# The second attention's projections as four products of 64 rows and 64 columns in two banks, with queries and keys sent apart

## The reference, cut to what matters

```python
def _L1_attn_ref(x, Wqkv, bqkv, Wr, br):        # x: [16, 512, 256], H = 16 heads of HE = 16
    xh = x.reshape(b, c, h, he).transpose(0, 2, 1, 3)
    qkv = jnp.einsum('bhce,ef->bhcf', xh, Wqkv) + bqkv      # Wqkv: [16, 48], the same for every head
    q, k, v = jnp.split(qkv, 3, axis=-1)
    att = jnp.einsum('bhqe,bhke->bhqk', q, k) / jnp.sqrt(jnp.float32(he))
    mask = jnp.tril(jnp.ones((c, c)), k=-1)
    att = jax.nn.softmax(att * mask, axis=-1)               # masked scores are 0, not left out
    out = jnp.einsum('bhqk,bhke->bhqe', att, v)
    return out.transpose(0, 2, 1, 3).reshape(b, c, d) @ Wr + br
```

## Time and profile before

| what | value |
|---|---|
| median of 3 runs | 2801.84 us (2799.59 to 2802.47) |
| profiled execution | 2797.78 us |
| its span | 2796.0 us |
| TensorE busy | 2615.3 us (94%) |
| VectorE, ScalarE, GpSimd busy | 2280.6, 2078.2, 1811.9 us |

### The profile page before, as it was taken

One profiled execution on the slowest core, in us unless ns is written; L12 is line 12 of the kernel. 1 busy time (PEld: TensorE's weight loads), 2 busy tenths in 40 slices (PEclk: granted clock), 3 DMA queues, 4 the chain that ended last, 5 costly groups with the idle time before them and its releaser, 6 DMA issues. The chain is left out here.

```text
span 2796.0 us, 75274 instructions
## 1 busy us (share of the span) xinstructions
PE 2615.3 (94%) x27044; PEld 1818.8 (65%) x27044; DVE 2280.6 (82%) x6931; ACT 2078.2 (74%) x3782; POOL 1811.9 (65%) x3152
## 2 busy tenths in 40 slices
PE   5999999999999999997889789999999999699999
PEld 3677777777777777775333257777777777466766
DVE  5999999999999999986655468888888888488998
ACT  4998899999998999895333257667677776478886
POOL 3767666777667766774421157677777767588885
PEclk8999999999999999999899889999999999899999
DMA  4334433444334433441000166655556664000001
GB/s 116 68 62 77 79 61 62 74 80 79 61 64 80 73 61 62 72 72 47 10 0 1 32 106 105 105 96 104 97 101 97 104 99 71 1 16 24 24 24 39
DMA packets 110387, 182.21 MB, mean 65 GB/s; under 512 B 27008, under 2 KB 96384, under 8 KB 97920
## 3 DMA queue, kind: packets, MB, share of 16 engines
q1 hardware_dynamic: 106560, 176.61, 34.7%
q10 hardware_dynamic: 3456, 0.79, 0.2%
HBM read 116.25 MB, written 60.29 MB: 63 GB/s over the span
## 5 line engine op out<-in xcount | busy, mean ns | idle before, releaser
L808 POOL TENSOR_TENSOR ratio_scores<-ratio_scores,ratio_max_cols 128x512 f32<-128x512 f32 (+3 forms) x1024 | 726.1, 726 | 319.3 <-DVE ratio_max_cols L718 316.9
L1328 DVE CUSTOM_DVE_ANT_0 zeroed_unused<-bank,zeroed_drop 128x512 bf16<-128x512 f32 (+3 forms) x1024 | 440.0, 484 | 121.1 <-PE bank L198 120.9
L198 PE MATMUL bank<-ratio_k_stack,ratio_q_stack 102*128 102x512 bf16 (+7 forms) x2048 | 506.3, 303 | 33.4 <-DVE ratio_max_cols L718 17.5
L718 DVE CUSTOM_DVE_ANT_0 ratio_scores<-bank,ratio_scores 128x512 f32<-128x512 f32 (+3 forms) x1024 | 472.4, 489 | 22.2
L1216 ACT ACTIVATE zeroed_prob<-bank 128x512 f32<-128x512 f32 x640 | 370.1, 593 | 161.2 <-PE bank L1103 160.3
L580 ACT ACTIVATE ratio_prob<-bank 128x512 f32<-128x512 f32 x640 | 378.4, 592 | 105.5 <-PE bank L494 102.7
L708 DVE TENSOR_TENSOR ratio_scores<-bank,ratio_inverse 128x512 f32<-128x512 f32 x640 | 435.9, 681 | 16.8 <-PE bank L198 9.6
L491 PE MATMUL bank<-const_f_sb,ratio_scores 128*128 128x128 f32 x2560 | 409.9, 274 | 0.9 <-ACT ratio_prob L580 0.9
L569 ACT ACTIVATE ratio_inverse<-bank 128x512 f32<-128x512 f32 x640 | 381.1, 596 | 12.7 <-PE bank L201 12.6
L573 ACT ACTIVATE ratio_inverse<-ratio_inverse 128x1024 f32<-128x1024 f32 x320 | 338.6, 1058 | 10.1
L1446 POOL TENSOR_SCALAR_AFFINE_SELECT zeroed_prob<-zeroed_prob 128x256 f32<-128x256 f32 (+1 forms) x640 | 227.7, 361 | 178.0 <-ACT zeroed_prob L1216 172.2
(11 more groups left out here) (178 smaller groups left out, 5412.6 us busy)
## 6 DMA issues: line engine op xcount, KB each, us to landing
ratio_q_stack<-ratio_parts_q SPq DMA_DIRECT2D x186, 128.0 KB
ratio_k_stack<-ratio_parts_k SPq DMA_DIRECT2D x186, 128.0 KB
zeroed_q_stack<-zeroed_parts_q SPq DMA_DIRECT2D x186, 128.0 KB, 4.7
zeroed_k_stack<-zeroed_parts_k SPq DMA_DIRECT2D x186, 128.0 KB, 7.7
ratio_parts_q<-ratio_parts SPq DMA_DIRECT2D x96, 128.0 KB
ratio_parts_k<-ratio_parts SPq DMA_DIRECT2D x96, 128.0 KB
zeroed_parts_q<-zeroed_parts SPq DMA_DIRECT2D x96, 128.0 KB
zeroed_parts_k<-zeroed_parts SPq DMA_DIRECT2D x96, 128.0 KB
```

The lines of the kernel that those rows point to most:

```text
L198: i = e.matmul(bank[:, off:off + w], qs[0:rows, s, hh, ib * P:(ib + 1) * P], ks[0:rows, s, hh, 0:w], start=(k == 0), stop=mask is None, sk ...
L718: i = e.tensor_tensor_reduce(seg, dot_banks[n % 2][:, at], seg, 1.0, 0.0, ALU.mult, ALU.max, mx[:, pair % M_BUFS, c:c + 1])
L808: i = e.tensor_tensor(seg, seg, mx[:, pair % M_BUFS, c:c + 1].to_broadcast([P, w]), ALU.subtract)
L1328: i = e.tensor_tensor_reduce(unused[:, n % 2, at], bank[:, at], drop[:, L - (ib + 1) * P:L], 1.0, 0.0, ALU.add, ALU.max, mx[:, pair % FOLD ...
```

## The change

- `project` issues four products of 64 rows and 64 columns: the weight's two diagonal blocks (heads 0 to 3, heads 4 to 7) times the two halves of the tokens. Heads 0 to 3 go to `prep_bank`, heads 4 to 7 to `o_bank`, the bank of the attend step; the first 256 tokens to partitions 0 to 63, the others to partitions 64 to 127. `values` issues eight products with 64 rows, a 128-column stationary operand and 64 moving columns, into the same two banks.
- Readers of these results read two banks, in two instructions each: ScalarE's and VectorE's `split`, VectorE's `values`.
- The products wait until the groups begun before them have been copied out of `o_bank`, and the attend step waits until projections issued before it have been read.
- The parts lie differently in their tile (tokens over partitions, heads over columns), so `send_parts` issues six DMAs of 64 partitions for a side, in runs of 512 bytes.
- SyncE gathers the queries before it sends the keys: send queries, gather queries, send keys, gather keys.
- New slots: queries of the half after the next at 13, keys of the next half at 3 (before: 11 and 15 for the half after the next), values at 5 (3), turns at 8 and 11 (6 and 9), suffix sums at 17 (19), tails at 9 (7). For half 1: queries at slot 1 and keys at 3 (before 1 and 5). ScalarE and VectorE do their steps of the split ahead of the rest of their preparation; the steps still follow one slot apart.

```diff
-Z_ROOT_AT, Z_XN_AT, Z_TURN_AT, Z_VALUES_AT, Z_SUFFIX_AT = 0, (3, 6), (6, 9), 3, 19
-Z_SPLIT_AT, Z_REST_AT, Z_MID_AT, Z_LO_AT = (11, 15), (12, 16), (13, 17), (14, 18)
+Z_ROOT_AT, Z_XN_AT, Z_TURN_AT, Z_VALUES_AT, Z_SUFFIX_AT, Z_SPLIT_AT = 0, (5, 8), (8, 11), 5, 17, (13, 3)
+Z_REST_LAG, Z_MID_LAG, Z_LO_LAG = 1, 2, 3
+QUARTER = HALF // 2
-Z_SECOND_AT, Z_SECOND_REST_AT, Z_SECOND_MID_AT, Z_SECOND_LO_AT = (1, 5), (2, 6), (3, 7), (4, 8)
-Z_TAILS_AT = 7
+Z_SECOND_AT = 1
+Z_TAILS_AT = 9
...
+def split_at(n, halves):
+
+    half, at = divmod(n, HALF_UNITS)
+    if n == Z_SECOND_AT:
+        return 1, 0
+    if at == Z_SPLIT_AT[0] and half + 2 < halves:
+        return half + 2, 0
+    if at == Z_SPLIT_AT[1] and half + 1 < halves:
+        return half + 1, 1
+    return None, None
...
+    two_banks = lambda n: max(prep[use] for slot, use in order if use[0] in "qkv" and slot <= n)
+    groups_before = lambda n: max(-((ZEROED_LAG + Z_ATTEND_AT[0] - n) // N_UNITS), 0)
...
+        quarters = ((prep_bank, slice(0, P // 2)), (o_bank, slice(P // 2, P)))
...
-            def project(half, side):
+            def project(half, side, n):
+
                 q.wait_ge(w.sem, w.loaded)
                 q.wait_ge(s["prep_read"], prep[sides[side], half] - 1)
-                e.matmul(prep_bank[:, :], w.w_in[:, side, :], xnT[:, half % 2, :], start=True, stop=True).then_inc(s["prep_filled"])
+                q.wait_ge(s["o_group"], groups_before(n))
+                for bank, heads in quarters:
+                    for k in range(2):
+                        i = e.matmul(bank[k * 64:(k + 1) * 64, 0:L // 2], w.w_in[heads, side, heads],
+                                     xnT[heads, half % 2, k * L // 2:(k + 1) * L // 2], start=True, stop=True, skip_group_check=True)
+                i.then_inc(s["prep_filled"])
...
-            def values(half):
+            def values(half, n):
                 q.wait_ge(s["prep_read"], prep["v", half] - 1)
+                q.wait_ge(s["o_group"], groups_before(n))
                 for t in range(T):
-                    i = e.matmul(prep_bank[:, t * P:(t + 1) * P], xnT[:, half % 2, t * P:(t + 1) * P], w.w_in[:, 2, :],
-                                 start=True, stop=True)
+                    for bank, heads in quarters:
+                        i = e.matmul(bank[:, t * 64:(t + 1) * 64], xnT[heads, half % 2, t * P:(t + 1) * P], w.w_in[heads, 2, heads],
+                                     start=True, stop=True, skip_group_check=True)
                 i.then_inc(s["prep_filled"])
...
                     q.wait_ge(s["o_group"], g)
+                    q.wait_ge(s["prep_read"], two_banks(n))
                     attend(e, g, part, o_bank, values_ones, prob, FOLD_PROBS, STACKS).then_inc(s["attended"])
...
-                e.activation(parts[:, side, 0, :], prep_bank[:, :], ACT.Identity, bias=w.bias_qk[:, side:side + 1]).then_inc(s["hi"])
+                for k, (bank, _) in enumerate(quarters):
+                    i = e.activation(parts[:, side, 0, k * L // 2:(k + 1) * L // 2], bank[:, 0:L // 2], ACT.Identity,
+                                     bias=w.bias_qk[:, side:side + 1])
+                i.then_inc(s["hi"])
...
-                e.scalar_tensor_tensor(out=rest[:, :], in0=prep_bank[:, :], scalar=w.bias_qk[:, side:side + 1],
-                                       in1=parts[:, side, 0, :], op0=ALU.add, op1=ALU.subtract).then_inc(s["prep_read"])
+                for k, (bank, _) in enumerate(quarters):
+                    cols = slice(k * L // 2, (k + 1) * L // 2)
+                    i = e.scalar_tensor_tensor(out=rest[:, cols], in0=bank[:, 0:L // 2], scalar=w.bias_qk[:, side:side + 1],
+                                               in1=parts[:, side, 0, cols], op0=ALU.add, op1=ALU.subtract)
+                i.then_inc(s["prep_read"])
...
                 for part in range(3):
-                    e.dma_start(part_dram[side][half % 2][part].rearrange("d h t -> h d t"),
-                                parts[:, side, part, :]).then_inc(s[f"parts_{sides[side]}"], 16)
+                    for k in range(2):
+                        to = part_dram[side][half % 2][part][:, :, k * L // 2:(k + 1) * L // 2]
+                        e.dma_start(to.rearrange("d (m h) t -> h d m t", m=2),
+                                    parts[k * 64:(k + 1) * 64, side, part, :]).then_inc(s[f"parts_{sides[side]}"], 16)
...
             for half in range(1, halves):
-                send_parts(half, 0)
-                send_parts(half, 1)
-                gather(half, slice(0, HALF), gathered(half)[0])
+                for side in range(2):
+                    send_parts(half, side)
+                    gather(half, side, slice(0, HALF), gathered(half)[0])
```

More of the change, by code:

```diff
@@ L1147, in pe @@
             turn_x(0, 1)
[L1148 to L1150 removed]
+            project(0, 0, -1)
+            project(0, 1, -1)
+            values(0, -1)
             suffix_sums(0)
@@ L1363, in prepare @@
                         normal(half // 2 + 1, Z_XN_AT.index(at))
-                if half + 2 < halves and at in Z_REST_AT:
-                    split(half + 2, Z_REST_AT.index(at))
             normal(0, 0)
@@ L1377, in dve @@
                     maxima(n)
+                split_half, side = split_at(n - Z_REST_LAG, halves)
+                if split_half is not None:
+                    split(split_half, side)
                 if half < halves:
@@ L1470, in pool @@
                     split_maxima(pair - 1)
+                split_half, side = split_at(n - Z_LO_LAG, halves)
+                if split_half is not None:
+                    split(split_half, side)
                 if half < halves:
```

88 lines of the change are left out of this document (40 added, 48 removed).

## The result

The changed kernel took 2913.4 us (median of 4 runs, 2908.7 to 2920.5) against 2800.7 for the kernel before on the same chip: ratio 1.0406, 95% interval 1.038 to 1.0431, 4% slower. Forecast was 2823 with a range to 2847: the direction was right, the size far off. The profiled execution's span is 2914.9 us. The other stages are as before to within 5 us; from the first dots of the second attention to its last it is 884.7 us (1604.89 to 2489.55), before 770.9 (1604.32 to 2375.22). A steady half takes 27.1 to 27.6 us in 15 of 26 cases and up to 29.4 in the others, 27.67 on the mean, before 24.24.

A forecast was written before the change was run, and what follows sets the result against it. TensorE was taken to set the pace, busy 195.2 of 200 us. Terms of +0.65 a half gave +20, late keys +6, the start -5: +21 on 2801.8, so 2823 us, range 2787 to 2847 (the forecast's own 2808 to 2838).

The forecast's parts named there:

- Projections: Query and key projections on TensorE: 0.67 us each to the next product, a gain of 0.21 each, 0.42 a half.
- rival C: The four quarters of a projection don't run together: +0.23 instead of -0.21 each, 2851 us; chance 0.05.
- Values: Value products on TensorE, 16 records of 64 columns: 1.11 us, +0.17 a half.
- The stall of TensorE: Values at slot 5 wait for VectorE's remainder of the keys projected at slot 3: 1.2 us a half.
- The vanished waits (-0.4): Other TensorE waits disappear as ScalarE and VectorE catch up during the stall: -0.4 us a half (0 to -1.1).
- The reads in two at 0: ScalarE and VectorE read two banks in two instructions; both have slack, so their throughput costs 0.
- The wait for the group's copy: Projections wait until the group accumulated in the same bank is copied out: +0.1 us a half (0 to 0.4).
- The way of the keys: Keys from projection through send and gather to the stack: 21.7 us, late, taken as +6 us in all (0 to +26).
- Rival B: Keys' gather ends last in every half, which becomes 25.7 us: 2842 us; chance 0.13.
- The send: SyncE's six DMA issues for a side, 3.7 us, and the time until the gather begins: 6.1 us together.
- The start: Half 1 waits less because queries are gathered while keys are split: -5 us (-11 to +2).

The follow-up runs named there:

- slots_only: The changed kernel's slots and queue order with the products, reads, values, single bank and three-DMA sends of the kernel before; 2832.3 us, ratio 1.0122.
- early_parts: The changed kernel with each bf16 part sent when its own engine has written it, same six DMAs a side; 2842.5 us, ratio 1.0141.
- old_sends: The changed kernel with the parts sent in three DMAs of 128 partitions and 1024-byte runs a side, as before; 2844.4 us, ratio 1.0164.
- six_long: The changed kernel with six DMAs a side of 64 partitions, but one run of 1024 bytes a partition; 2902.0 us, ratio 1.0352.
- heads_first: The changed kernel with the parts laid out in DRAM by head, so the sends' outermost dimension is 64 rows; 2872.1 us, ratio 1.0256.

## Why the prediction was wrong

**Projections: right.** Forecast 0.67 us from start to next product, measured 0.60 (1917.10 to 1917.70); the four quarters run together, so rival C falls. **Values: right.** Forecast 1.11, measured 1.05.

**The stall of TensorE: right in place and size.** 1.16 us in the half shown, 37.0 over 31, released by VectorE's remainder (forecast 1.2).

**The vanished waits (-0.4): wrong.** The 53.5 us that the term drew on are waits of the weight loads. TensorE's own products waited 9.7 us for exponentials before, 0.3 a half, and 11.7 after:

```profile
PE bank L1103 <- ACT zeroed_prob L1216: 9.7, 31, 0.3
```

The wait of the weight loads did fall (to 22.3) and gave nothing: with the new slots and the old products (slots_only) it fell as well (to 23.7), and a half is 1.16 longer. **The reads in two at 0: wrong,** 0.25 a half. **The wait for the group's copy: 8.3 us in 30,** 0.28 and not 0.1. The measured terms add up to -0.56 + 0.11 + 1.19 + 0.28 + 0.25 = +1.27 a half; the pace of the engines in early_parts is 25.60, +1.36, where the forecast had +0.65.

**The way of the keys: the step that failed.** Late keys were put at +6 us (0 to +26). Making the keys arrive in time gave back 69 to 71 us (old_sends, early_parts). The text counted 21.7 us, found the keys late by its own count, and then took +6 of +26, because "a late gather at slot 0 takes the place of other waits and my chain leans high". Both reasons were wrong. The chain did not lean high: 7.76 (forecast 8.0), 7.45 (6.1) and 7.70 (7.6) are 22.9. And a late gather is not a delay to be set against other waits: since slot 3 of a half projects the keys for slot 0 of the next, the way and four slots form a closed chain, and the half cannot be shorter than their sum. Rival B said so, with 25.7 and 2842, which is the forecast's own count without the discount from 26 to 6; it had a chance of 0.13 and the send 1.35 too short. With the measured 27.1 it would have given 2802 + 31 x 2.9 = 2892. The rest is the early halves 1 to 3 (22.1 each before, 25.6 to 28.6 now), the last one (21.9 before, 27.5 now) and steady ones that are longer than the chain shown; what makes these longer was not traced.

**The send: mis-sized.** The issues were nearly as forecast (3.5 us for six, forecast 3.7). The time behind the last was taken from the kernel before, 2.44, and is 3.95, because half as many DMA engines carry it: with 4 heads outermost it is long whatever the runs (six_long), and with 64 rows outermost it is 1.5 (heads_first). The Trainium skill's rule that the prediction weighed ("DMA: Bandwidth & Descriptors", "Rules for kernel authors": two transfers to disjoint partition halves share the engines) holds here in its advice and not in its reason: here neither half used all engines (share 0.25 to 0.27).

**The start: right mechanism, wrong sum.** -5 became +1.4. The keys' send was expected at about 1620 and begun at 1623.84, behind the issues of the queries' gather, and took 8.92 us to its gather instead of 6.1. With the old sends the term is -5.0 (29.4 for 34.4).

**TensorE's clock: missed.** In 24 of 31 halves (19 of the 26 steady ones) the granted clock falls to its lower level (1.2 GHz), as in the stretch 1921.90 to 1925.00 above (0.50), which begins some 2 us after the idle time ahead of the values: the attend of 1923.56 takes 1.79 instead of 1.08. What makes it fall is not shown. The idle time alone does not: slots_only has it in every half, and its clock stayed at the upper level from 1636 to 2430; with early_parts it fell in 2 of the 26 halves. It cost nothing on top here: of the changed kernel's halves 4 to 29, the 19 with it last 27.69 us on the mean and the 7 without it 27.60, which fits a pace set by the chain of the keys. Where the engines set the pace, one fall costs 0.84 us (old_sends: 26.03 for 25.19).

## What to carry to other kernels

When a step is moved to the half directly before its use, write the chain from it through DRAM back to itself and divide by the number of periods that lie between the step and its use: that is a floor of the period, not one wait among others. When a count says late, discount it only with a row that shows what absorbs it. Read a DMA's outermost dimension on both sides before splitting it; the DMA share of the stretch behind its issue says how many engines carry it, as long as packets are in flight all the time. A wait of the weight loads under running products is no slack that a stall can use up.

## What the runs showed of the hardware that I had not expected

A store of 64 KB with 4 heads outermost moved at 73 to 79 GB/s with a share of about a quarter of the engines, one of 128 KB with 8 heads at 171 and 0.51, one with 128 rows at 243 and 0.87, packets of 512 bytes included. At its shortest, an issue of such a store took 0.55 to 0.60 us of SyncE whether it had 64 or 128 partitions (3.30 and 3.50 for six, 1.80 for three), and 0.48 with 128 rows outermost (1.44 for three). With 64 rows outermost it took 0.64 to 0.82 (heads_first), and the issues then held the stores to 97 GB/s. Four products of 64 rows by 64 columns and 256 columns cost 0.60 us where one of 128 by 128 with 512 cost 0.88, so about 0.16 us of the ideal gain of 0.44 (half of 0.88) is lost.
